# A graph network on one core: edge logits through a DRAM table instead of one-hot matmuls, and two plain gathers added on VectorE

## What is computed

```python
h = relu(layernorm(x))
feat = concat([h[src], h[dst]], axis=1)             # 8192 x 2048
e_hh = relu(feat[:256]      @ W_hh + b_hh)          # 2 tiles of 128 edges
e_oo = relu(feat[256:1536]  @ W_oo + b_oo)          # 10 tiles
e_ho = relu(feat[1536:]     @ W_ho + b_ho)          # 52 tiles
logit = concat([e_hh, e_oo, e_ho]) @ W_a + b_a      # one number an edge
alpha = softmax of logit over the edges of one dst
z   = segment_sum(alpha * h[src], dst)
x1  = x + relu(concat([h, z]) @ W_hn or W_on + b)
out = x1 + graph convolution of relu(layernorm(x1)) with W, b
```

## Time and profile before

| | before |
|---|---|
| median of 3 runs | 665.55 us (665.29 to 667.62) |
| span of the profiled execution | 665.7 us |
| mean granted clock of TensorE | 0.938 |
| TensorE busy | 571.4 us, 86% |
| VectorE busy | 442.1 us, 66% |
| ScalarE busy | 287.4 us, 43% |
| GpSimd busy | 217.7 us, 33% |
| DMA, moved | 140.53 MB, mean 211 GB/s |

### The profile page before, as it was taken

One profiled execution on the slowest core, in us unless ns is written; L12 is line 12 of the kernel. 1 busy time (PEld: TensorE's weight loads), 2 busy tenths in 40 slices (PEclk: granted clock), 3 DMA queues, 4 the chain that ended last, 5 costly groups with the idle time before them and its releaser, 6 DMA issues.

```text
span 665.7 us, 8504 instructions
## 1 busy us (share of the span) xinstructions
PE 571.4 (86%) x2440; PEld 424.7 (64%) x2441; DVE 442.1 (66%) x903; ACT 287.4 (43%) x466; POOL 217.7 (33%) x228
## 2 busy tenths in 40 slices
PE   0899999999949995969697998667949999879987
PEld 0788777776626674647475666434738788768876
DVE  6715266775776987867878975686795289872152
ACT  2623312113175554547473555589853182142110
POOL 2000230186775766667653676310030000000000
PEclk9899999999969997988989899788978899989989
DMA  8335483499999999999999999983455076030021
GB/s 316 129 111 175 135 307 122 150 224 323 301 298 314 291 314 299 310 305 317 298 318 281 323 295 308 257 226 111 128 198 213 16 247 228 2 126 0 1 79 48
DMA packets 54727, 140.53 MB, mean 211 GB/s; under 512 B 6050, under 2 KB 6178, under 8 KB 54690
## 3 DMA queue, kind: packets, MB, share of 16 engines
q0 software_dynamic: 20624, 74.98, 41.7%
q1 hardware_dynamic: 25824, 50.34, 21.8%
q10 hardware_dynamic: 8242, 14.75, 5.9%
HBM read 123.27 MB, written 16.78 MB: 210 GB/s over the span
## 4 chain that ended last, share of the span: by engine, by line
PE 42%; DMA 23%; POOL 12%; issue 10%; DVE 8%; ACT 3%; POOLq 1%; DVEq 0%
PE ps L646 23%; DMA gath<-tab_a,tabl_s 19%; POOL gath L315 7%; PE ps L632 6%; POOL gath L308 3%; PE ps L826 3%; DMA gath<-tab_b,tabl_s 3%; PE ps L596 3%; PE ps L782 2%; POOL tabl_s L305 2%; ACT onehot L495 2%; PE ps L803 2%; DVE logit_d L947 1%; DVE logit_d L1036 1%; PE ps L625 1%
## 5 line engine op out<-in xcount | busy, mean ns | idle before, releaser
L646 PE MATMUL ps<-ring_h,actT_h 128*128 128x512 f32 x520 | 228.3, 439 | 34.4 <-ACT stage L466 15.8
L646 PE MATMUL ps<-ring_h,actT_l 128*128 128x512 f32 x520 | 209.0, 402 | 0.0
L646 PE MATMUL ps<-ring_l,actT_h 128*128 128x512 f32 x520 | 208.4, 401 | 0.0
L495 ACT ACTIVATE onehot<-onehot,lgs 128x512 bf16<-128x512 bf16 x192 | 124.6, 711 | 104.2 <-DVE onehot L929 104.2
L646 PEld LDWEIGHTS ps<-ring_h,actT_h 128*128 128x128 f32 x520 | 101.6, 195 | 68.1 <-ACT stage L466 17.7
L315 POOL DMA_INDIRECT gath<-tab_b,tabl_s x64 | 105.7, 1652 | 95.8 <-DMA gath<-tab_a,tabl_s 40.4
L448 ACT CAST ring_h<-raw 128x512 fp32r<-128x512 f32 x160 | 94.8, 614 | 87.8 <-PE ps L646 70.7
L912 DVE SCALAR_TENSOR_TENSOR gath<-gath,wa_b 128x1024 f32<-128x1024 f32 x64 | 78.0, 1219 | 67.6 <-DMA gath<-tab_b,tabl_s 67.6
L897 DVE TENSOR_TENSOR ring_l<-raw,ring_h 128x512 fp32r<-128x512 f32 x160 | 106.6, 685 | 16.5 <-ACT ring_h L448 16.4
L646 PEld LDWEIGHTS ps<-ring_h,actT_l 128*128 128x128 f32 x520 | 101.0, 194 | 22.9
L646 PEld LDWEIGHTS ps<-ring_l,actT_h 128*128 128x128 f32 x520 | 101.8, 196 | 20.9
(11 more groups left out here) (160 smaller groups left out, 517.3 us busy)
## 6 DMA issues: line engine op xcount, KB each, us to landing
raw<-in_L_gnn_W_ho_dram SPq DMA_DIRECT2D x32, 256.0 KB, 3.9
raw<-in_L_gnn_W_oo_dram SPq DMA_DIRECT2D x32, 256.0 KB, 6.8
raw<-in_L_gnn_W_hh_dram SPq DMA_DIRECT2D x32, 256.0 KB, 7.3
raw<-in_L_gnn_W_on_dram SPq DMA_DIRECT2D x32, 256.0 KB, 4.8
raw<-in_L_gnn_W_hn_dram SPq DMA_DIRECT2D x32, 256.0 KB, 4.0
tab_a<-stage ACTq DMA_DIRECT2D x24, 256.0 KB, 7.4
tab_b<-stage ACTq DMA_DIRECT2D x24, 256.0 KB, 8.1
w1row<-in_L_gnn_W_dram SPq DMA_DIRECT2D x2, 2048.0 KB, 8.9
```

The costliest lines, as they stand in the source:

```text
L495: ins = nc.scalar.mul(onehot[:, s, 1 + i, :], onehot[:, s, 1, :], lgs[:, i, q:q + 1])
L646: mm = nc.tensor.matmul(ps[:, first + m, :], w, v, start=(k == 0 and i == 0), stop=(k == KT - 1 and i == 2))
```

## The change

It does two things. The logits no longer go through matmuls. A DRAM table `pair_d` with one float for each (kind, dst, src) is filled with -1e30 at the start; when the logits of a tile are there, GpSimd scatters the 128 values (4 bytes each) to it by a third column of indices; when a kind is complete its 1 MB is loaded back as `logit_d`. A scatter waits for the one before it to have landed. Masks, inverse counts, bf16 parts, logit one-hots and their matmuls are gone; the counting matmuls stay. And the rows of `tab_b` are no longer added by the DMA: both rows are gathered plainly, without a wait between them, into two rings of five slots (`gath_a`, `gath_b`), and VectorE adds them (`edge_sum`) before the sum over columns (`edge_dot`). Index columns are read from `tabl_i` directly. The edge tiles stand three in four steps from step 38 to step 122.

```diff
-        GB = 8
-        gath = sb("gath", [P, GB, D], F32)
+        GA = 5
+        gath = sb("gath", [P, 8, D], F32)
+        gath_a = sb("gath_a", [P, GA, D], F32, over="gath")
+        gath_b = sb("gath_b", [P, GA, D], F32, over="gath", shift=4 * GA * D)
+        pair_d = nc.dram_tensor("pair_d", [3 * N * N, 1], F32).ap()
@@ GpSimd
+            for t in range(3):
+                pool.dma_start(pairs[t].rearrange("(p m) s -> p (m s)", p=P), stage[:, :, :].rearrange("p m s -> p (m s)")).then_inc(s_fill, 16)
-            def gather_src(q, s, kinds):
-                pool.wait_ge(s_edge, q + 1)
-                nc.gpsimd.tensor_copy(tabl_s[:, s, :], tabl_i[:, bass.ds(q, 1), :].rearrange("p a b -> p (a b)")).then_inc(s_stg, 1)
-                pool.wait_ge(s_stg, q + 1)
-                pool.sem_inc(s_seen, 1)
-                pool.indirect_dma_start(out=gath[:, s, :], ... in_=tab_a[0:kinds * N, :], ...).then_inc(s_ga[s], 16)
-            def gather_dst(s, u, kinds):
-                pool.wait_ge(s_ga[s], u * 16 + 16)
-                pool.sem_inc(s_seen, 1)
-                pool.indirect_dma_start(out=gath[:, s, :], ... in_=tab_b[0:kinds * N, :], ...
-                                        compute_op=ALU.add).then_inc(s_g[s], 16)
+            def gather_src(q, kinds):
+                pool.wait_ge(s_edge, q + 1)
+                pool.indirect_dma_start(out=gath_a[:, q % GA, :], ... in_=tab_a[0:kinds * N, :], ...).then_inc(s_ga[q % GA], 16)
+            def gather_dst(q, kinds):
+                if q >= GA:
+                    pool.wait_ge(s_sum, q - GA + 1)
+                pool.indirect_dma_start(out=gath_b[:, q % GA, :], ... in_=tab_b[0:kinds * N, :], ...).then_inc(s_gb[q % GA], 16)
+            def scatter(q):
+                pool.wait_ge(s_edge, GA + q + 1)
+                t = kind_of(q)
+                if q > FIRST_OF[t]:
+                    pool.wait_ge(s_sc[t], 16 * (q - FIRST_OF[t]))
...
+                pool.indirect_dma_start(out=pair_d, out_offset=bass.IndirectOffsetOnAxis(ap=tabl_i[:, q, 2:3], axis=0),
+                                        in_=lg[:, q:q + 1], in_offset=None).then_inc(s_sc[t], 16)
+            def logits_back(t):
+                pool.wait_ge(s_sc[t], 16 * TILES[t])
+                pool.dma_start(logit_d[:, t, :, :], pairs[t].rearrange("(m p) s -> p m s", p=P)).then_inc(s_lg[t], 16)
+            for q in range(GA, ET):
...
+                scatter(q - GA)
+                gather_src(q, 1 + kind_of(q))
+                gather_dst(q, 1 + kind_of(q))
+                if q == T_HO + T_OO - 1:
+                    logits_back(0)
+            for q in range(ET - GA, ET):
+                scatter(q)
+            logits_back(1)
+            logits_back(2)
-        SUM_AT = {(6 + i, k): i * TC + k for i in range(6) for k in range(TC)}
...
+        EDGE_STEPS = [38 + q * 4 // 3 for q in range(ET)]
@@ VectorE
+            def edge_sum(q):
+                i = q % GA
+                dve.wait_ge(s_ga[i], q // GA * 16 + 16)
+                dve.wait_ge(s_gb[i], q // GA * 16 + 16)
+                nc.vector.tensor_tensor(gath_a[:, i, :], gath_a[:, i, :], gath_b[:, i, :], ALU.add).then_inc(s_sum, 1)
+                    for e in EDGES_AT.get((q, k), ()):
+                        edge_sum(e)
+                        if e:
+                            edge_dot(e - 1)
+            edge_dot(ET - 1)
+            for t in range(3):
+                dve.wait_ge(s_lg[t], 16)
+                ins = nc.vector.tensor_reduce(mx3[:, t, :], logit_d[:, t, :, :], AX.X, ALU.max)
@@ TensorE
-            with pe.Fori(0, 6) as i:
-                edge_chunk(i + 6, before=lambda k: uniform_sums(i, k))
+            with pe.Fori(0, 6) as i:
+                edge_chunk(i + 6)
```

More of the change, by code:

```diff
@@ L172, in gnn_kernel @@
         s_topl = [sem(f"top_loaded{m}") for m in range(NM)]
-        s_mask = sem("masks_ready")
-        s_part = sem("onehot_parts_ready")
+        s_neg = sem("empty_pairs_made")
+        s_fill = sem("pairs_filled")
+        s_sc = [sem(f"logits_scattered{t}") for t in range(3)]
+        s_lg = [sem(f"logits_loaded{t}") for t in range(3)]
         s_pool = sem("pool_chain")
@@ L226, in gnn_kernel, with kind_of @@
         TILES = (T_HO, T_OO, T_HH)
+        FIRST_OF = (0, T_HO, T_HO + T_OO)
+        def kind_of(q):
+            return 0 if q < T_HO else 1 if q < T_HO + T_OO else 2
         CH_EDGE = 3 * 2 * NN
@@ L321, in tables_landed @@
                     pool.wait_ge(s_st[i], 64 * kinds)
[L323 to L334, removed]
             for i in range(4):
                 pool.wait_ge(s_st[i], 32)
-            for q in range(GB):
-                gather_src(q, q, 1)
+            for q in range(GA):
+                gather_src(q, 1)
             tables_landed(1)
-            pool.wait_ge(s_copied, NM + NM * 4)
-            for q in range(GB - LAG):
-                gather_dst(q, 0, 1)
+            for q in range(GA):
+                gather_dst(q, 1)
             bias(0, b_hh)
[L344 to L359, removed]
+            pool.wait_ge(s_fill, 48)
+            for q in range(GA, ET):
+                if q == T_HO:
+                    tables_landed(2)
+                if q == T_HO + T_OO:
+                    tables_landed(3)
+                scatter(q - GA)
[7 more added lines that the diff above has]
+            logits_back(2)
+            pool.wait_ge(s_ohu, OS + ET)
             for i in range(4):
@@ L386, in gnn_kernel @@
         LAST_COUNTS = FIRST_COUNTS + ET // (2 * KT) - 1
-        SUM_AT = {(6 + i, k): i * TC + k for i in range(6) for k in range(TC)}
[L390 to L410, removed]
-        LAST_OF_KIND = (T_HO - 1, T_HO + T_OO - 1, ET - 1)
+        EDGE_STEPS = [38 + q * 4 // 3 for q in range(ET)]
+        EDGES_AT = {}
+        for q, at_step in enumerate(EDGE_STEPS):
+            EDGES_AT.setdefault(divmod(at_step, KT), []).append(q)
         def is_a(q):
@@ L609, in open_banks @@
                     nc.tensor.matmul(ps[:, b, :], zeros_r[:, 0:P], zeros_r[:, :], start=True, stop=False, skip_group_check=True)
-            def open_masked(t):
-                pe.wait_ge(s_mask, t + 1)
-                for b in range(NM):
-                    nc.tensor.matmul(ps[:, b, :], ident_b[:, :], mask_b[t][:, b, :], start=True, stop=False, skip_group_check=True)
             def close_banks(done):
@@ L735, in _ @@
                     free = lambda m: pe.wait_ge(s_copied, waits[c] + (m if c == 0 else 0))
-                chunk(q + c, NM, ms, free, before=lambda k: last_sums(q + c, k))
-            pe.wait_ge(s_kfree, 3 * NM)
+                chunk(q + c, NM, ms, free)
+            pe.wait_ge(s_ccopy, 3)
             q += 4
```

185 lines of the change are left out of this document (53 added, 132 removed).

## The result

The changed kernel takes 705.93 us (median of 4 runs, 703.0 to 708.67) against 666.59 us for the kernel before in the same session. The ratio is 1.0575, 95% interval 1.053 to 1.062: slower by 5.8%. The span of its profiled execution is 704.9 us, 39.2 us over the 665.7 of before.

The account below looks back on a forecast made before the run. DMA engines were taken as the bound, before and after, at 4.43 then 4.27 us a tile: last rows at 417 us, plus 21 to the maxima, 21 to the next matmuls and 168.4 to the end, 627 us; range 600 to 670.

Parts of the forecast that it names:

- What bounds the kernel before: The stage with the gathers, until the last tile is taken at 446.9 us, is bound by DMA engines.
- the price of the accumulate: In the gather stage an accumulating gather costs 2.6 us of DMA time, a plain one 1.45; the change saves 68 us.
- The scatter's price to the DMA engines: In the loop, writing 128 values of 4 bytes costs the DMA engines 0.4 us a tile.
- Rival 4: In the loop a scatter costs the engines a full row's time per value, 1.45 us a tile: 680 us; chance 0.14.
- two tiles in 8.1 us, 4.05 us a tile: GpSimd's loop, waiting for the previous scatter with two tiles in flight, stays under 4.43 us a tile; nothing charged.
- The 2.3 us for a lone scatter: A scatter alone on GpSimd's queue lands about 2.3 us after its issue, from a least gather landing of 3.7 us.
- Rival 3: The loop waits: landings take 7 us, not 5.4, giving 4.85 us a tile, 649 us; at 8 us, 676; chance 0.10.
- The cover: Slack in the loop between the scatter wait's 4.05 us a tile and DMA's 4.43: 0.4 us a tile.
- GpSimd's issue: GpSimd issues three DMAs a tile at 0.97 us each, 2.9 us a tile against 3.82 us before.
- The tail: From the last rows to the maxima 21 us: last scatters 3 us apart, landed at +12.4, then load and reduction.
- VectorE and TensorE under the bound: In the loop VectorE needs 3.4 us and TensorE 3.67 us a tile, both under the DMA pace.
- the first add at 141 us: On VectorE the first add of gathered rows, placed at step 38, comes at about 141 us.

Follow-up runs that it names:

- e4: The kernel before with its second gather made plain, overwriting the rows of the first instead of adding to them: 621.71 us, ratio 0.9335.
- e1: The changed kernel without its 64 scatters; the table keeps its fill and is still loaded back: 602.54 us, ratio 0.9047 to the kernel before.
- e9: The changed kernel with the scatter of a turn issued behind the two gathers of that turn instead of ahead: 706.73 us, ratio 1.056 to the kernel before.
- e2: The changed kernel with four DRAM tables in turn, each scatter waiting for the one four before, only one table loaded back: 651.98 us, ratio 0.979.
- e7: The changed kernel with two tables for even and odd tiles (one for hh), larger taken on VectorE, sum right behind the add: 638.15 us, ratio 0.953.
- e3: The changed kernel with a tile's sum over columns right behind its add, ahead of the next add: 691.50 us, ratio 1.038 to the kernel before.
- e6: The kernel before, keeping one-hot logits, with two plain gathers into four-slot rings and the add on VectorE, no scatters: 672.26 us, ratio 1.007.

## Why the prediction was wrong

Forecast 627 us with 600 to 670, measured 705.9, and 0.14 for slower. By its own steps:

- *What bounds the kernel before* was right, and so was the price of the accumulate: taken at 2.6 against 1.45 us, a plain gather took 1.43 us in e4 and 1.32 in e1, and making only the second gather plain gave 44 us.
- *The scatter's price to the DMA engines*, taken at 0.4 us, is next to nothing: a lone scatter's packets are 1.1% of 2.15 us of sixteen engines, 0.02 us, by the row shown under e9. The q0 rows of after give 106.0 us for 36.46 MB, 34.8 tiles, 3.05 us a tile, against 2.86 us for two gathers at e4's price and 2.64 at e1's; what is over is in the gathers' own packets. Rival 4, the slower one, was the wrong mechanism. The Trainium skill (DMA: Bandwidth & Descriptors, Specifications) says that transfers under 512 bytes are done as read-modify-write, and its section Bandwidth has 0.68 us for 4 KB over 128 partitions. By that figure the scatters would have cost 14 us, an estimate; the packets here don't show it.
- **The step that failed** is "two tiles in 8.1 us, 4.05 us a tile. That is under 4.43, so I charge nothing for it". I followed the rows from issue to landing and took the scatter as an addition of 0.4 us to them. But every turn holds one scatter's whole flight and the wake-up of 0.73 us behind it. A turn of 4.05 us leaves 3.3 us for the flight; between 200 and 400 us it measured 4.7 us in the mean, behind two thirds of a tile of gathers in the queue. Flight and wake-up make 5.4 us, the waits for late logits 22.3 / 63 = 0.35 us more, and 35 turns took those 200 us, 5.7 us each; over the whole loop it is 5.53. The prediction had the place right, "in the same queue behind the gathers issued before it", and had the time of it wrong.
- *The 2.3 us for a lone scatter* came near by luck: the last two of the five at the end of the queue, with nothing about, landed after 2.13 to 2.15 us. It was worked out from 3.7 us, taken from the earlier trace rows as the least landing of a gather. That is the landing of a plain load of x, which goes to the same tile at the start of the run; gathers of `tab_a` take 4.6 us at the least. By the same working they would have given 3.2 us. The landings in the kernel before of the loads of x and of the gathers of `tab_a`:

```profile
DMA to landing us min/median/max: 3.7/5.2/6.5
...
DMA to landing us min/median/max: 4.6/14.5/18.5
```

- *Rival 3* had the right place, a tenth of the chance. Its quantity, rows that land after 7 or 8 us, does occur (7.2, 8.2 and 8.8 us are the longest in the chain from 200 to 480 us), but its price at 8 us, 5.35 us a tile and 676 us, was still too low. Its sums also take all 53 tiles from 4.43 us, though 20 of them stood at 4.27, which is 3 us.
- The cover was called 0.4 us a tile. It was gone, and what the wait for the scatter before cost was 5.53 - 4.70 = 0.83 us a tile by e2, 52 us over 63 tiles, and 0.81 us by e7 against e3.
- *GpSimd's issue*, 2.9 us a turn, was mis-sized. The 0.97 us came from a direct DMA behind an indirect one. Two indirect ones stand 1.24 to 1.3 us apart at the least, 0.94 to 1.0 busy and 0.30 idle. In e2 a turn of three takes 4.3 us in the shown rows and 4.70 in the mean. With this alone the forecast would have been 4.7 us a tile in place of 4.43 and 4.27, 33 x 0.27 + 20 x 0.43 = 17 us later.
- *The tail* was 25.4 us for 21: the last five scatters started 2.9 to 5.5 us apart in place of 3.0, because the first landed after 4.8 us behind the last gathers and the next two after 3.3 and 3.2 us beside weight loads. *VectorE and TensorE under the bound* was right (120 and 147 of 200 us busy), and so was the first add at 141 us and the 189.4 us from the maxima to the end (190.3).

The sum of the misses: last tile at 489.2 for 417, 72.2 us; tail 4.4 us; the rest 0.9 us; 77.5 us from 627.4 to 704.9.

What stays open is how the 2.7 us that a scatter takes longer under gathers divide between its place in the queue and the load on the engines. The packets show that the place matters; how much a scatter ahead of the gathers would save, no run shows, since none has that order. Scatters with no order among them in one table were not tried, since their writes may fall on the same place.

## What to carry to other kernels

A transfer that costs the engines next to nothing can still set the pace if the next one of its kind waits for it to land and other work stands behind that wait in the issuing engine's queue: the turn is its issue to its landing under load plus the wake-up, so take the landing from rows with the same load, and never from a lone one. Two destinations in turn took most of the wait away here for two more loads of 1 MB and two maxima, and with the sum right behind its add (14 us by e3) turned a kernel 5.8% slower into one 4.7% faster. Before a run is built to compare two orders in a loop, write out the order over two turns: e9's was the order that stood there already. Before moving an add from the DMA engines to VectorE, count what VectorE already does in the same stretch: without its one-hots the add was hidden (e1: 171 of 200 us busy at 3.99 us a tile), with them (e6) it took back all that the DMA engines had gained.

## What was not expected of the hardware

A plain indirect DMA costs GpSimd 0.94 to 1.0 us of busy time at the least and 0.30 us of idle before the next indirect one, so about 1.25 us, and 1.4 to 1.6 in the mean under load (e7, e1, e2). A scatter of 128 x 4 bytes took 2.1 us from issue to landing with nothing about, and its packets kept their place behind all gather packets issued before it. With plain gathers alone the DMA engines moved 396 GB/s over 200 us (e1), against 300 GB/s at a full share with every second gather accumulating.
